# Column maxima of a two-layer perceiver: masked columns stored in pairs of keys, and another order of TensorE's and ScalarE's work around them

## What is computed

```python
qh, kh, vh = heads(norm(x) @ Wq.T + bq), heads(ctx @ Wk.T + bk), heads(ctx @ Wv.T + bv)   # 16 heads of 16
logits = einsum('bhqd,bhkd->bhqk', qh, kh) / 4
logits = logits + mask * -1e9          # first layer only
attn = softmax(logits, axis=-1)
out = einsum('bhqk,bhkd->bhqd', attn, vh)
x = x + merge(out) @ Wo.T + bo
```

## Time and profile before

| | |
|---|---|
| median of 3 runs | 1459.7 us (1459.39 to 1460.17) |
| the profiled execution | 1467.39 us, its span 1465.3 us |
| TensorE matmul busy | 1239.3 us (85%) |
| TensorE weight load busy | 895.6 us (61%) |
| VectorE busy | 989.7 us (68%) |
| ScalarE busy | 854.7 us (58%) |
| GpSimd busy | 656.4 us (45%) |
| granted TensorE clock, mean | 0.971 |
| first cross attention, first to last row maximum | 564.4 us |

### The profile page before, as it was taken

The page is one execution under the profiler, slowest core; times in us unless marked ns, Lnnn a source line. Parts: engine busy times, 40 slices in busy tenths (PEclk is TensorE's granted clock), DMA queues, the critical chain, the costliest instruction groups (busy, mean ns, idle before and its releaser), DMA issues. The chain is left out here.

```text
span 1465.3 us, 32532 instructions
## 1 busy us (share of the span) xinstructions
PE 1239.3 (85%) x12658; PEld 895.6 (61%) x12658; DVE 989.7 (68%) x1543; ACT 854.7 (58%) x1373; POOL 656.4 (45%) x897
## 2 busy tenths in 40 slices
PE   5888888878888878798888889999989998898887
PEld 3555556556556655555564566766666677766654
DVE  3777777777777777548567677667675667766674
ACT  3565656656656555455365567667766766666331
POOL 2554544434545453323101444545474656654543
PEclk9999999999999999899999999999999998999999
DMA  4211211211111130210063202101201122200000
GB/s 154 85 52 52 71 51 52 71 51 52 52 51 52 51 116 2 61 48 1 2 211 114 79 30 59 67 22 51 57 33 41 40 59 59 59 2 2 5 8 18
DMA packets 32853, 78.49 MB, mean 54 GB/s; under 512 B 4416, under 2 KB 16448, under 8 KB 28480
## 3 DMA queue, kind: packets, MB, share of 16 engines
q1 hardware_dynamic: 32704, 76.42, 17.1%
HBM read 69.07 MB, written 7.34 MB: 52 GB/s over the span
## 5 line engine op out<-in xcount | busy, mean ns | idle before, releaser
L697 POOL TENSOR_TENSOR ca_fold<-ca_probT 128x512 f32<-128x512 f32 x128 | 163.8, 1280 | 268.7 <-ACT ca_probT L927 268.3
L936 ACT ACTIVATE ca_probT<-bank 128x512 f32<-128x512 f32 x256 | 140.5, 595 | 114.2 <-PE bank L830 113.1
L801 PE MATMUL bank<-ca_kT,ca_q_blk 32*128 32x512 f32 x512 | 149.7, 661 | 27.7 <-DVE ca_probT L1012 25.2
L919 ACT ACTIVATE ca_prob<-ca_neg_logit,ca_neg_max 128x1024 f32<-128x1024 f32 x64 | 73.6, 1150 | 160.8 <-DVE ca_neg_max L986 160.8
L830 PE MATMUL bank<-ident,ca_prob 128*128 128x128 f32 x1024 | 149.5, 288 | 12.3 <-DVE ca_picked L1024 5.3
L807 PE MATMUL bank<-ca_q_blk,ca_kT 32*128 32x128 f32 x2048 | 153.8, 290 | 0.0
L927 ACT ACTIVATE ca_probT<-ca_probT 128x1024 f32<-128x1024 f32 x128 | 135.4, 1057 | 30.0 <-DVE ca_probT L1012 25.1
L739 PE MATMUL bank<-ca_ctxT,ca_wk 128*128 128x512 f32 x256 | 134.0, 623 | 9.1 <-DMA ca_bk<-in_L_xattn_bk 9.1
L755 PE MATMUL bank<-ca_wv,ca_ctxT 128*128 128x256 f32 x512 | 134.0, 386 | 4.1 <-DVE ca_q L955 1.2
L830 PEld LDWEIGHTS bank<-ident,ca_prob 128*128 128x128 f32 x1024 | 113.7, 145 | 33.4 <-DVE ca_picked L1024 7.1
L847 PEld LDWEIGHTS bank<-ca_probT,ca_v 128*32 128x32 f32 x4096 | 111.1, 112 | 36.9 <-ACT ca_v L909 18.9
(11 more groups left out here) (324 smaller groups left out, 2707.0 us busy)
## 6 DMA issues: line engine op xcount, KB each, us to landing
ca_ctxT<-in_ctxT SPq DMA_DIRECT2D x16, 1024.0 KB, 5.3
ctxT<-in_ctxT SPq DMA_DIRECT2D x16, 1024.0 KB, 4.8
ca_mask_i<-in_mask SPq DMA_DIRECT2D x32, 256.0 KB, 6.4
ek_ctxT<-in_ctxT SPq DMA_DIRECT2D x12, 512.0 KB, 6.2
early_k<-ek_out SPq DMA_DIRECT2D x48, 128.0 KB, 4.0
ca_kT<-early_k SPq DMA_DIRECT2D x12, 512.0 KB, 5.8
ca_mask_col_i<-in_mask_keys SPq DMA_DIRECT2D x16, 256.0 KB, 6.6
lat<-in_x SPq DMA_DIRECT2D x1, 1024.0 KB, 4.9
```

Source lines behind the costliest of these rows:

```text
L697: pool.tensor_tensor(f[:, :, :], p[:, 0:4, :], p[:, 4:8, :], ALU.add).then_inc(self.fold_step, 1)
L801: mm = pe.matmul(self.core.bank[:, 2 + half, :], self.q_blk[rows, b % 2, u, :, :], self.kT[rows, b % 2, u, :], start=True, stop=True, tile ...
L936: self.banks.free(act.activation(self.probT[:, n % 2, 4 * h:4 * h + 4, 2 * (s % 2) + 1, :], self.core.bank[:, x, :].rearrange("p (n q) -> ...
```

## The change

Three things are changed. In the first layer the masked columns are stored with the keys of two neighbouring chunks side by side: the add L971 writes every second element (a step of 8 bytes), the reduction L977 reads two neighbours and then steps on, over both axes at once, and the subtraction L1007 reads every second element. In the first layer TensorE's list has the whole value projection ahead of turn_column_max and the whole key projection between it and spread_top, and ScalarE copies the values ahead of the row exponentials. In the second layer the value projection keeps its two halves around turn_column_max; spread_top follows directly; the causal heads and the transposes of the feed-forward input, which stood ahead of the values, and the causal scores, back transpose and output, which stood between the values and the keys, follow it, and then the whole key projection.

```diff
--- before.py
+++ after.py
@@ -612,7 +612,7 @@
             self.neg_logit = sb("neg_logit", [P, CTX])
             self.mask_col_i = sb("mask_col_i", [P, NCH, S], I32)
             self.mask_col = sb("mask_col", [P, 2, NCH, S])
-            self.masked_col = sb("masked_col", [P, NCH, P])
+            self.masked_col = sb("masked_col", [P, NCH // 2, P, 2])
             self.masked_ready = sem("masked_ready")
             self.mask_loaded, self.mask_ready = sem("mask_loaded"), sem("mask_ready")
         else:
@@ -968,14 +968,16 @@
                 dve.wait_ge(self.mask_ready, 2 * b + 2)
             if s >= 1:
                 self.banks.wait_taken(dve, ("spread", s - 1))
-            dve.tensor_tensor(self.masked_col[:, :, :].rearrange("p c (e q) -> p c e q", q=S),
-                              scores.rearrange("p c (e q) -> p c e q", q=S),
-                              self.mask_col[:, b % 2, :, :].unsqueeze(2).broadcast_to([P, NCH, 2, S]), ALU.add)\
-                .then_inc(self.masked_ready, 1)
+            dve.tensor_tensor(self.masked_col[:, :, :, :].rearrange("p a (h q) e -> p a e h q", h=2),
+                              scores.rearrange("p (a e) (h q) -> p a e h q", e=2, h=2),
+                              self.mask_col[:, b % 2, :, :].rearrange("p (a e) q -> p a e q", e=2).unsqueeze(3)
+                              .broadcast_to([P, NCH // 2, 2, 2, S]), ALU.add).then_inc(self.masked_ready, 1)
             dve.wait_ge(self.masked_ready, s + 1)
-            scores = self.masked_col[:, :, :]
-        dve.tensor_reduce(self.column_max[:, y, :], scores.rearrange("p c q -> p q c"), AX.X, ALU.max)\
-            .then_inc(self.column_max_ready, 1)
+            dve.tensor_reduce(self.column_max[:, y, :], self.masked_col[:, :, :, :].rearrange("p a q e -> p q a e"),
+                              AX.XY, ALU.max).then_inc(self.column_max_ready, 1)
+        else:
+            dve.tensor_reduce(self.column_max[:, y, :], scores.rearrange("p c q -> p q c"), AX.X, ALU.max)\
+                .then_inc(self.column_max_ready, 1)
 
     def row_maxima(self, dve, s):
         b, y = s // GROUPS, s % 2
@@ -1004,8 +1006,10 @@
         x = self.banks.wait_filled(dve, ("spread", s))
         tops, shape = self.core.bank[:, x, 0:P], [P, NCH, P]
         if self.masked:
-            self.banks.free(dve.tensor_tensor(self.columns(s), self.masked_col[:, :, :],
-                                              tops.unsqueeze(1).broadcast_to(shape), ALU.subtract), ("spread", s))
+            self.banks.free(dve.tensor_tensor(self.columns(s).rearrange("p (a e) q -> p a e q", e=2),
+                                              self.masked_col[:, :, :, :].rearrange("p a q e -> p a e q"),
+                                              tops.unsqueeze(1).unsqueeze(1).broadcast_to([P, NCH // 2, 2, P]),
+                                              ALU.subtract), ("spread", s))
         else:
             self.banks.free(dve.tensor_copy(self.tops_row[:, :], tops), ("spread", s))
             self.banks.wait_taken(dve, ("spread", s))
@@ -1085,17 +1089,13 @@
                     pe.wait_ge(ca.masked_ready, STEPS)
                     early.project(pe, END_PIECES[0], END_BANKS)
                 if s + 2 < STEPS:
-                    ca.project_v(pe, s + 2, parts=(0,))
+                    ca.project_v(pe, s + 2)
                 if s < STEPS:
                     ca.turn_column_max(pe, s)
-                if s + 2 < STEPS:
-                    ca.project_v(pe, s + 2, parts=(1,))
                 if s + 4 < STEPS:
-                    ca.project_k(pe, s + 4, parts=(0,))
+                    ca.project_k(pe, s + 4)
                 if s < STEPS:
                     ca.spread_top(pe, s)
-                if s + 4 < STEPS:
-                    ca.project_k(pe, s + 4, parts=(1,))
                 for x in range(3):
                     if 6 <= s - IW_STEPS[x] < 9:
                         ffn_weights.transposes_on_tensor(pe, x, s - IW_STEPS[x] - 6)
@@ -1169,10 +1169,10 @@
             for s in range(STEPS + 1):
                 if s >= 1:
                     ca.take_t(act, s - 1)
+                if s + 2 < STEPS:
+                    ca.take_v(act, s + 2)
                 if s < STEPS:
                     ca.exponentials(act, s)
-                if s + 2 < STEPS:
-                    ca.take_v(act, s + 2)
                 if s + 4 < STEPS:
                     ca.take_k(act, s + 4)
                 if s < STEPS:
@@ -2338,27 +2338,24 @@
                     ca.transposes(pe, s - 1)
                 for t in tile_at(s, 3):
                     sa.latent_transposes(pe, t, norm1.xn_ready)
-                for t in tile_at(s, 8):
-                    sa.heads(pe, t)
-                for t in tile_at(s, 17):
-                    ff.latent_transposes(pe, t)
                 if s + 2 < STEPS:
                     ca.project_v(pe, s + 2, parts=(0,))
                 ca.turn_column_max(pe, s)
                 if s + 2 < STEPS:
                     ca.project_v(pe, s + 2, parts=(1,))
+                ca.spread_top(pe, s)
+                for t in tile_at(s, 8):
+                    sa.heads(pe, t)
+                for t in tile_at(s, 17):
+                    ff.latent_transposes(pe, t)
                 for t in tile_at(s, 5):
                     sa.scores(pe, t)
                 for t in tile_at(s, 9):
                     sa.back(pe, t)
                 for t in tile_at(s, 10):
                     sa.output(pe, t)
-                late_keys = 8 <= s + 4 < STEPS and (s + 4) // 4 not in early.BATCHES
-                if late_keys:
-                    ca.project_k(pe, s + 4, parts=(0,))
-                ca.spread_top(pe, s)
-                if late_keys:
-                    ca.project_k(pe, s + 4, parts=(1,))
+                if 8 <= s + 4 < STEPS and (s + 4) // 4 not in early.BATCHES:
+                    ca.project_k(pe, s + 4)
                 for x in range(3):
                     if s in FW_TRANSPOSE[x]:
                         weights.transposes_on_tensor(pe, x, FW_TRANSPOSE[x].index(s))
```

## The result

The changed kernel takes **1369.86 us**, the median of 4 runs (1366.37 to 1375.21), against 1459.93 us for the kernel before (4 runs, 1459.39 to 1460.3). The ratio is 0.9386, with a 95% interval of 0.9356 to 0.9417. The prediction was 1364 us with a range of 1344 to 1402. The profiled execution took 1370.36 us, its span 1368.3 us, at a mean granted clock of 0.983.

The account below looks back on a forecast made before the run. A loop of waits through several engines, none full, was taken as the bound. Savings of 85 us in the first layer and 10 in the second took the profiled 1467.4 to 1372, less 7.7 to the median 1364 us, range 1344 to 1402.

Parts of the forecast that it names:

- Step 1, pairs: First layer: reading neighbours in pairs cuts VectorE's reduction from 1.93 to 1.22 us, reduction start to turn 1.29 instead of 2.00.
- Rival A: Every jump still costs, so pairs save half: first-layer reduction 1.58 us, 22 us more, total 1386, chance 13%.
- rival B: Pairs do not help the first layer's reduction, which stays at 1.93 us: 43 us more, total 1407, chance 5%.
- Step 2, steps of 8 bytes: First layer: add and subtraction on every second element stay at 1.22 us each, against 1.93 if the step costs.
- Rivals C and E: First-layer add and subtraction each 0.71 us dearer: total 1431, chance 5%; with the reduction unhelped too, 1469, chance 2%.
- Step 3, the order: First layer, TensorE: second value half fits in idle time with 0.1 us to spare; 0.95 us leaves the loop after the spread.
- Step 4, the loops: First layer: steps take 6.06 us without the product with the values, 7.98 with it; a pair 14.04 instead of 17.17.
- Step 5, ScalarE's copy: First layer: the value copy (0.57 us) ahead of the row exponentials falls in idle time and costs nothing.
- What was given back: First layer: 12 us lost, namely 7 for weight preparation, 4 for transposed weights holding banks, 1 for the queries' second half.
- Second layer: Order alone: 18.5 us won by earlier spreads, 8.5 lost, mostly waits behind the moved heads; net 10 us less.
- Rival D, a new wait: First layer: ring of three banks delays the value projection, 0.5 us missing in each step: 32 us more, total 1396, chance 8%.
- The term that was off: Whole kernel: the profiled execution's 7.7 us above the median was carried over, turning 1372 into a median of 1364 us.

Follow-up runs that it names:

- experiment 2: The changed kernel with masked columns stored as before, so only the engine orders of both layers change: 1417.72 us, ratio 0.9678.
- experiment 5: The changed kernel with four neighbouring chunks side by side instead of two, so add and subtraction step by 16 bytes: 1459.51 us, ratio 0.9986.
- experiment 3: The changed kernel with ScalarE's value copy again behind the row exponentials in the first layer: 1372.34 us, ratio 0.9375.
- experiment 8: The changed kernel with GpSimd's mask conversion one step later in the first layer, away from VectorE's rounding of weights: 1369.45 us, ratio 0.9364.
- experiment 1: The kernel before with only the layout in pairs, both layers in the old order: 1415.93 us, ratio 0.9678.

## Why the prediction was right

The forecast case came true, and its first layer by its own steps. That the totals fit as closely as they do is in part luck: both layers were helped by the clock.

- *Step 1, pairs*: 1.22 us forecast, 1.220 measured. Rival A (1.58) and rival B (1.93) are out. Rival B's price, 43 us more, was right: the change without the faster reduction is experiment 2, with a first layer 42.3 us longer and a ratio that makes 1412.9 us of 1459.9. Its total of 1407 was too low by what the main forecast was too low.
- *Step 2, steps of 8 bytes*: free, 1.22 to 1.23. Rivals C and E are out as the change stands; experiment 5 shows that their mechanism exists at 16 bytes, where it took the whole gain.
- *Step 3, the order*: experiment 2 gives 43.4 us of the first layer to it, 37.2 in the 56 steps without a dip. The second value half does fit with 0.1 us to spare: in the timeline the turn starts without a wait.
- *Step 4, the loops*: 6.16 and 8.07 us against 6.06 and 7.98. The two tenths have places. The add follows the start of the subtraction after 1.36 us (398.98 to 400.34) where I had 1.22 + 0.03, and what follows the spread comes after 0.20 (404.77 to 404.97), where I had 0.11. Over the layer that is 6 us: some 90 instead of 97.
- *Step 5, ScalarE's copy*: costs nothing, as said. It also brings next to nothing (experiment 3), which I had not said and later, in the expectation of that experiment, denied.
- *What was given back*: 12 us forecast. Steps with weights or queries stand above the ordinary 6.16 and 8.07 by some 10 us in all, if steps 8, 20 and 30 are counted without the dips that the trace before had in them. Part of this has another cause than I gave: some 4 us are the collision of experiment 8, not VectorE's missing slack.
- So the first layer's 85.65 us against 85 hides two misses and a gift: 90 instead of 97, 10 instead of 12, and about 5 us from clock dips that the one profiled execution had and the other had not.
- *Second layer*: 10.3 us against 10, and this fit is in large part luck. The causal scores gave 9.9 in six steps (11 forecast for seven), the key steps 7.2 in all (7.5 forecast). The heads cost 5.5 where I had 7.5 (six times 1.2 is 7.2), by exactly the wait named. Two terms are not in the sum and nearly cancel. Steps 48, 49 and 62 gave 3.7 through the clock. The steps behind a key copy cost 4.1: I counted the plain key steps as gain, and did not ask what the later key copy pushes on ScalarE.
- *Rival D, a new wait* of 0.5 us in every step: not there. ScalarE's copy of the values waits for TensorE and not the reverse.
- *The signs*: the second layer's spreads were to come some 0.8 us after the end of the row maxima. They come 0.34 after it in most steps. TensorE's wait for the column maxima was to be near 10 us and is 16.2.

**The term that was off** is the last one: "That execution is 7.7 above the median 1459.7, so the median becomes 1364." The profiled execution of the changed kernel, 1370.36, is within 0.5 us of its own median. The 7.7 us of before go with the clock (its mean was 0.971; other executions of that kernel on a chip of these comparisons took 1459.9 at 0.977 and 1465.95 at 0.972). Of them 4.8 are the dips in steps 8, 20 and 30 (these steps fell by 2.2 to 2.4 us in experiment 1, every ordinary one by 0.7), which the changed kernel's trace lacks, and experiment 1's too. No trace shows an execution of the kernel before at 1460 us, so where the rest lay, and that these dips are missing there, is not shown. From profile to profile the time fell by 97.0 us (95 forecast), from median to median by 90.1. The median missed 1364 by 5.9 us: 7.2 of the offset were not there and 0.7 is the rounding of 1364.7, less 2.0 by which the profile gained more than forecast. Without the 4.8 and 3.7 us that the clock gave the two layers, they would have gained some 88 us and not 96.

## What to carry to other kernels

If a VectorE operation is slower on SBUF than on the same shape in PSUM, look at its step, and change the layout so that every access comes in neighbours of two; then check that the writer and every other reader stay at a step of 8 bytes or less, since at 16 bytes the price came back here. When an operation is moved in one engine's list, follow the copy that frees its bank to its new place on the copying engine, and then ask what stands behind that copy: here both losses of the second layer, the one forecast and the one not, lay in ScalarE's order. Moving the value copy gave the first back in the time; moving the column exponentials gave most of the second back in the steps concerned, and moved part of it to others. An offset between a profiled execution and the median is worth reading before it is carried over: where the clocks of the two differ, it belongs to the waits of that kernel and may go with them.

## What the runs showed of the hardware

For 1024 float32 elements per partition on VectorE: a reduction over a step of 512 bytes in SBUF takes 1930 to 1951 ns, over pairs or fours of neighbours 1220; an element-wise operation with a step of 8 bytes 1223 to 1231, writing or reading, and with 16 bytes 2076 writing and 2091 reading. The 16-byte step is thus dearer by 0.14 us than the reduction's 512-byte one, which I had not expected.

A float32 to bfloat16 tensor_scalar of VectorE from SBUF to SBUF went from 1.28 us to 3.08 us for six instructions when GpSimd worked beside it (conversion and then a fold): two of the six lasted until GpSimd's operation ended, the others took 0.28 to 0.32. Additions and reductions of VectorE beside the same conversion stayed at 1.22 to 1.27.

Two executions of the same instructions differed by 2.4 us in one step, through the granted clock after TensorE had stood for 1.1 to 1.9 us twice in a row. It is left open what decides whether the clock falls there; no run was made for it. In the second layer's old order the clock was low in the same steps of all three traces that have it (0.76 in step 48, behind a wait of 1.92 us before the scores), and it was 1.00 in step 48 of every trace with the new order: an order that takes a wait of TensorE away can gain by the clock of the next step too.
